# The scan of the linear branch in the causal stage, cut into two halves of 512 columns in consecutive steps

## The reference

```python
qkv = (x @ Wqkv_w + Wqkv_b).reshape(Bb, Ll, 3, Hh, dd)      # 16 heads of 8
...
attn = jax.nn.softmax(scores + causal_mask, axis=-1)
y_softmax = jnp.einsum('bhij,bhjd->bhid', attn, v)
retention = 1.0 - jax.nn.sigmoid(Lambda_raw)
k_stp = k * scale
def step(state, inp):
    q_t, k_t, v_t = inp
    hebbian = v_t[..., :, None] * k_t[..., None, :]
    state = retention * state + Gamma * hebbian
    y_t = jnp.einsum('bhij,bhj->bhi', W_static + state, q_t)
    return (state, y_t)
...
y = alpha * y_softmax + (1.0 - alpha) * y_stp
```

## Time and profile before

| | |
|---|---|
| median of 3 runs | 1887.36 us (1886.95 to 1887.83) |
| the profiled execution | 1888.6 us, span 1887.3 us |
| mean granted clock of TensorE | 0.957 |
| busy: PE, DVE, ACT, POOL | 1647.2, 1276.3, 1113.8, 689.8 us |
| scan L1457 | 32 instructions, 73.8 us |

### The profile page before, as it was taken

How to read it: one execution, slowest core, us unless ns; L and a number is a source line. 1 busy time by engine, 2 the same in 40 slices (tenths; PEclk the granted TensorE clock), 3 DMA queues, 4 the chain that set the end, 5 groups by cost and what they waited for, 6 DMA issues and landing times. The chain is left out here.

```text
span 1887.3 us, 45037 instructions
## 1 busy us (share of the span) xinstructions
PE 1647.2 (87%) x19451; PEld 1016.3 (54%) x19472; DVE 1276.3 (68%) x2067; ACT 1113.8 (59%) x1654; POOL 689.8 (37%) x500
## 2 busy tenths in 40 slices
PE   4588888999999999999997778888888888899999
PEld 2355656777677767776774223333343343466665
DVE  4666746666666667666666868877877886765664
ACT  3265677766776676667662467667666767533221
POOL 4112202443444244424442265565655555411100
PEclk7699999999999999999997799999999999999999
DMA  6764100000000000000015146237226222000000
GB/s 177 201 152 117 28 15 1 2 2 2 1 2 2 2 1 2 2 2 1 2 64 131 36 140 150 69 102 169 69 85 163 69 69 69 23 6 12 6 12 12
DMA packets 38747, 102.27 MB, mean 54 GB/s; under 512 B 3944, under 2 KB 12288, under 8 KB 35284
## 3 DMA queue, kind: packets, MB, share of 16 engines
q1 hardware_dynamic: 37524, 93.09, 18.6%
q10 hardware_dynamic: 1024, 6.29, 1.7%
HBM read 67.12 MB, written 31.46 MB: 52 GB/s over the span
## 5 line engine op out<-in xcount | busy, mean ns | idle before, releaser
L1447 DVE TENSOR_REDUCE arena<-ring 128x2 f32<-128x1024 f32 (+2 forms) x320 | 342.1, 1110 | 89.0 <-PE ring L1304 62.3
L1547 ACT ACTIVATE arena<-ring 128x1024 f32<-128x1024 f32 (+1 forms) x320 | 291.3, 937 | 129.4 <-PE ring L1333 90.2
L1354 PE MATMUL accs<-arena 128*9 128x512 f32 (+3 forms) x1536 | 174.3, 528 | 2.7 <-ACT arena L1547 2.6
L1297 PE MATMUL ring<-arena 48*128 48x512 bf16 (+3 forms) x768 | 127.4, 343 | 42.7 <-DVE arena L1447 21.8
L1326 PE MATMUL ring<-arena 51*128 51x512 bf16 (+3 forms) x768 | 124.1, 341 | 45.6 <-DVE arena L1447 25.5
L2486 POOL TENSOR_TENSOR arena<-arena 128x1280 f32<-128x1280 f32 x28 | 65.3, 2332 | 266.5 <-PE accs L2256 235.1
L2470 POOL TENSOR_TENSOR arena<-arena 128x1024 f32<-128x1024 f32 x32 | 76.1, 2377 | 203.6 <-DVE arena L2346 203.6
L2478 POOL TENSOR_TENSOR arena<-arena 128x512 f32<-128x512 f32 x112 | 142.0, 1303 | 11.3 <-DVE arena L2327 11.3
L292 POOL TENSOR_SCALAR xn<-x,moments,rstd 128x128 f32<-128x128 f32 x80 | 64.3, 817 | 193.9 <-DVE rstd L263 178.3
L2753 ACT ACTIVATE arena<-ring 128x512 f32<-128x512 f32 x80 | 47.8, 597 | 147.3 <-PE ring L2608 140.5
L2713 DVE TENSOR_TENSOR arena<-arena,ring 128x512 f32<-128x512 f32 x80 | 55.0, 687 | 87.9 <-PE ring L2610 74.5
(11 more groups left out here) (345 smaller groups left out, 4269.6 us busy)
## 6 DMA issues: line engine op xcount, KB each, us to landing
arena<-whole_k SPq DMA_DIRECT2D x32, 512.0 KB, 4.7
arena<-whole_q SPq DMA_DIRECT2D x32, 512.0 KB, 6.3
arena<-c_scratch_q SPq DMA_DIRECT2D x14, 384.0 KB, 8.8
arena<-c_scratch_k SPq DMA_DIRECT2D x14, 384.0 KB, 11.9
a_scratch_k<-arena SPq DMA_DIRECT2D x8, 512.0 KB
c_scratch_k<-arena SPq DMA_DIRECT2D x8, 512.0 KB, 3.6
a_scratch_q<-arena SPq DMA_DIRECT2D x4, 768.0 KB, 3.6
arena<-a_scratch_q ACTq DMA_DIRECT2D x8, 384.0 KB, 6.5
```

Of the source, the lines that this page charges most:

```text
L1297: mm = nc.tensor.matmul(o[r], qs[half(r, SCORE), pair, n * P:(n + 1) * P], ks[half(r, SCORE), pair, a:c], start=True, stop=not diag)
L1354: mm = nc.tensor.matmul(acc[ci % 2][32 * h:32 * h + HD + 1, a - c * BANK:BANK], c_values[b % 2][:, j, r * HEADS // 2 + 2 * g + i, :], weig ...
L1447: nc.vector.tensor_reduce(dst, src, AX.X, ALU.max, negate=True).then_inc(c_max_taken.up(item), 1)
L1547: nc.scalar.activation(view(c_probs[wi % 4]), view(ps), ACT.Exp).then_inc(c_weights_made.up(item), 1)
```

## The change

The scan of 1024 columns becomes two of 512 columns. The second starts from the last column of the first, and waits on VectorE for the first to be over. The first stays where the scan was, the second is hung on the following step, in front of what that step already held for the scale. The scale waits for the second half. The planner keeps the old cost for the first half and charges nothing for the second, so the order of all other items is the same. `HALVES` is 2 and `BANK` is 512.

```diff
--- before.py
+++ after.py
@@ -1067,7 +1067,8 @@
                 for j in range(HD):
                     s = at + 6 * j
                     side[s + (j == 0)].append(("kv", b, j))
-                    side[s + 3 + (j == 0)].append(("scan", b, j))
+                    for h in range(HALVES):
+                        side[s + 3 + h + (j == 0)].append(("scan", b, j, h))
                     more = j < HD - 1
                     side[s + 4 + more].append(("scale", b, j))
                     side[s + 5 + more].append(("read", b, j))
@@ -1106,6 +1107,9 @@
                         return 0.00205 * cols, (), 0
                     n = len(score_pairs(c, j)[item[5]])
                     return n * (0.00077 * cols + (0.15 if a == j * P else 0)), (("A", 0.17 + 0.00166 * n * cols),), 1
+                if item[0] == "scan" and item[3]:
+
+                    return 0, (), 0
                 return TIMES.get(item[0], (0, (), 0))
 
             clock = {"P": 0.0, "A": 0.0, "D": 0.0}
@@ -1451,11 +1455,16 @@
                             nc.vector.tensor_tensor(late[:, :, 0, :], late[:, :, 0, :], late[:, :, 1, :], ALU.min).then_inc(
                                 c_max_joined.up((b, g)), 1)
                     elif kind == "scan":
-                        _, b, j = item
+
+                        _, b, j, h = item
                         sk = c_spread["k"][j % 2]
                         dv.wait_ge(c_kv_made, (b, j))
-                        nc.vector.tensor_tensor_scan(sk[:, :], c_retain[:, j:j + 1].to_broadcast([P, T]), sk[:, :], 0.0,
-                                                     ALU.mult, ALU.add).then_inc(c_state_made.up((b, j)), 1)
+                        if h:
+                            dv.wait_ge(c_state_made, (b, j, h - 1))
+                        cols = sk[:, h * BANK:(h + 1) * BANK]
+                        nc.vector.tensor_tensor_scan(cols, c_retain[:, j:j + 1].to_broadcast([P, BANK]), cols,
+                                                     sk[:, h * BANK - 1:h * BANK] if h else 0.0,
+                                                     ALU.mult, ALU.add).then_inc(c_state_made.up((b, j, h)), 1)
                     elif kind == "att":
                         _, b, p = item
                         view = ps[:, :].rearrange("p (n h c) -> p n h c", n=2, c=32)
@@ -1556,7 +1565,7 @@
 
                         _, b, j = item
                         sk = c_spread["k"][j % 2]
-                        ac.wait_ge(c_state_made, (b, j))
+                        ac.wait_ge(c_state_made, (b, j, HALVES - 1))
                         nc.scalar.activation(sk[:, :], sk[:, :], ACT.Identity, bias=w("c_static", j, j + 1),
                                              scale=w("c_gamma", j, j + 1)).then_inc(c_state_scaled.up((b, j)), 1)
                     elif kind == "tp" and item[2] < pairs:
```

## The result

The changed kernel takes 1903.47 us (median of 5 runs, 1899.24 to 1906.45), the kernel before beside it 1887.83 (5 runs, 1886.95 to 1890.93): 1.0059 times as long, with a 95% interval of 1.0038 to 1.0081. Forecast were 1890.4 and a range up to 1896. The loss is some 11 us by the ratio (with 7 to 15 in its interval) and 15.6 by the two medians; 3 were forecast. The profiled execution took 1899.67 us, its span is 1898.4, and the mean granted clock 0.947 against 0.957.

A forecast was written before the change was run, and what follows sets the result against it. It took the handing over of the ring's three PSUM buffers as the causal stage's bound. Batch 0 gave +0.15, batches 1 and 2 +0.40 each, batch 3 +2.04, together +3.0 us: 1890.4 us from 1887.36, range 1884 to 1896.

The forecast's parts named there:

- a half: Each 512-column scan on VectorE: 0.16 us fixed plus 1.06, so 1.22 us; carry read 0 to 0.16, taken as 0.
- adjacent pair: Two halves with nothing between end 2.48 us after the start instead of 2.28: +0.20 us for what waits behind.
- j = 0: First scan of a batch: later second half delays ScalarE's scale; +1.22 us in batches 1, 2, +1.24 in 3, +0.75 in 0.
- j = 1: Adjacent halves in batches 1 and 2: the reduction behind also waits for scores, so only +0.08 us each.
- j = 3, 5: Adjacent halves in batches 0 to 2: scores and ScalarE's scale wait behind the scan, so all of +0.20 us is paid.
- j = 4: GpSimd's cast is freed earlier by the shorter first half; TensorE's transposes of the maxima start 0.5 us earlier.
- j = 6: Same chain through GpSimd's cast: TensorE's transposes of the maxima start 0.8 us earlier, in batches 0 to 2.
- rival (b): Granted clock: three or four more stretches at 1.2 GHz cost 2.5 to 3.5 us, giving 1893.5 us; chance 0.20.
- own sign of being wrong: The prediction would be wrong if, among other signs, stretches at 1.2 GHz changed in number by more than three.
- Rival (a): Delay at j = 0 is absorbed, gains at j = 4 and 6 stay: 1886 us, down to 1883.5; chance 0.16.
- deciding point: Whether TensorE's scores L1297 behind the scale still start within 0.3 us of their old place relative to the scan.
- Rival (c): Gains and losses both end in slack, as VectorE, ScalarE and TensorE are under 85% busy: 1887.4 us; chance 0.22.

The follow-up runs named there:

- odd_only: Kernel before with only the scans of j = 1, 3, 5, 7 in halves, in consecutive steps: 1898.45 us, 1.0040 of before.
- same_j0w: Kernel before with the scans of j = 1 to 7 in halves, both in the same step, j = 0 whole: 1900.28 us, 1.0061 of before.
- j0_only: Kernel before with only the scan of j = 0 in halves, the other seven whole: 1895.25 us, 1.0034 of before.
- delay_small: Kernel before, no scan split, with a 16-column ScalarE copy between scan and scale of j = 0: 1891.92 us, 0.9999 of before.
- same_fill: same_j0w with W score matmuls repeated once or twice more ahead of two idle stretches of TensorE, units 2 and 3: 1895.99 us, 1.0032 of before.
- j46: Kernel before with only the scans of j = 4 and 6 of batches 0 to 2 in halves: 1889.06 us, 0.9996 of before.
- j46_fill: j46 with one W score of unit 3 formed twice more ahead of idle TensorE: 1886.60 us, 0.9976 of before.
- j0_whole: Changed kernel with the scan of j = 0 whole again, the other seven in halves: 1891.95 us, 1.0000 of before.

## Why the prediction was wrong

Point by point, against its own steps. "Measured" is the ledger of a steady batch, of changes that stand in both traces of the changed kernel.

| step | forecast | measured |
|---|---|---|
| a half | 1.22 us, carry read 0 to 0.16 | 1.215 first, 1.28 second half (medians) |
| adjacent pair | +0.20 | +0.25 |
| j = 0 | +1.22 (batch 0 +0.75) | +1.23 (+0.75 and +0.88) |
| j = 1 | +0.08 | +0.25 (+0.08, +0.18) |
| j = 2 | 0 | 0 |
| j = 3, 5 | +0.2 each | +0.25 each |
| j = 4 | -0.5 | -0.48 |
| j = 6 | -0.8 | -0.31 - 0.49, and +0.50 back at vT |
| j = 7 | 0 | 0 |
| sum | +0.40 | +1.2 |

**The direct terms** were read rightly but for j = 1 and the end of j = 6. Behind j = 3 and 5 the carry read shows, about 0.07 us. In rows, two adjacent halves of j = 5:

```profile
1325.64 2.54 DVE L1465 TENSOR_TENSOR_SCAN arena<-arena 128x512 f32<-128x512 f32 x2
```

2.54 against 2.28 for the whole scan. By the Trainium skill (VectorE: DVE Perf Modes, section on the DRAIN), which measured it on tensor_copy, the semaphore between them costs nothing extra; the pair would then cost one fixed part of 0.16 and the carry's 0.07, less 0.08 of overlap, 0.15 us. Measured are 0.26, so here the wait costs 0.11, near the 0.12 that the prediction had from rows 5 and 7.

The step on j = 6 had the right first waits but not the whole chain: half a microsecond of its gain ends at vT, because GpSimd's products set when L1733 runs, and they were not among the rows that I followed. Besides, 0.3 of the 0.8 is not the cast's: before, the join L1451 took 0.60 us there, to the end of a GpSimd product that had begun at 1329.59, and 0.17 after. In odd_only, where j = 6 is whole and the cast takes its 2.24 us, the ledger has the same -0.31. So that the two add up to the forecast 0.8 is luck for 0.3 of it. The Trainium skill, GPSIMD Engine Reference, section Specifications, says that GpSimd's SBUF interfaces are shared with VectorE and contend with instructions of two inputs from SBUF; these rows agree: the join has two such inputs and lasts until the product ends.

The sum of the local terms is about +0.5 in batch 0 (j = 1 can't be read there, the stretches at 1.2 GHz differ), +1.2 in each of 1 and 2, and +1.9 in batch 3 (1.23 for j = 0, 0.25 for j = 1, 0.46 for j = 3; forecast 2.04): +4.8 us for the forecast +3.0. That alone would have been 1892, in the range.

**The step that failed** is the one that kept the clock out of the sum and put it into rival (b) as "three or four more such stretches" at 0.85 us, with a chance of 0.20. By the granted clocks of all runs the changed kernel is at 1.2 GHz for 192 us and the kernel before for 168 to 169: 23 us more, seven stretches of 3.4. With 11 to 13 us of loss by the two ratios and 4.8 of local terms, 6 to 8 us are left for them, 0.9 to 1.2 us each; at the 0.29 us that the executions of one kernel show for 1 us at 1.2 GHz they cost 7 us. So the price was nearly right and the number half of what came; the prediction's own sign of being wrong, a change in number by more than three, came true. Rows 2 and 14 showed stretches at 1.2 GHz in a batch of before, and each place of the batch where the walk found a few tenths of a microsecond was a chance for one more. I had tied them to j = 0 alone. The runs show otherwise: odd_only and same_j0w leave j = 0 whole and have 188 and 192 us at 1.2 GHz, j0_only 174.

At one place the price stands by itself: behind j = 0 of batch 3. The changed kernel has a stretch there that the kernel before has in neither trace. The changed kernel, its copy and before:

```profile
1537.00:1540.40 3.40, 3.40 (x24) 1.18 (x23) 2.15 (x2) 1.23 (x2) 3.12 (x2) 0.50 0.01 2
```

```profile
1538.90:1542.30 3.40, 3.40 (x23) 1.18 (x21) 2.01 (x2) 1.09 (x2) 2.98 (x2) 0.50 0.01 2
```

```profile
1529.50:1532.90 3.40, 3.04 (x34) 1.76 (x26) 2.36 (x5) 2.02 (x5) 1.95 (x1) 1.00 0.02 5
```

In the ledger it costs 1.52 and 1.51 us. delay_small, with a hold of 0.25 us, has it too (+1.56). But so have three of the traces with a whole scan and no hold at j = 0 (same_j0w, same_fill, j46), so the hold isn't what it takes.

Over the fifteen kernels of the table the change against before goes with the mean time at 1.2 GHz, 0.47 us for each us of it (correlation 0.93). That slope holds the local delays too, which grow along with it, so it is no price of the clock by itself (the 0.29 within one kernel is nearer to that). That idle time brings the stretches, and not the other way round, rests on the fills, on the trace of j46_fill above all: three batches of three.

**Rival (a)**, the relief wins: half true and hidden. The gains exist, but in j46 they end as idle TensorE and 1.2 GHz; only with that idle time filled is the median clear of before. Its deciding point, whether L1297 (now L1301) behind the scale starts within 0.3 us of its old place relative to the scan, decided against it: it starts 5.73 us behind the scan's start where it was 4.50, 2.20 behind the scale's both times, so the hold was not absorbed. **Rival (c)**, all ends in slack: false for the change, true for delay_small and j0_whole.

What stays open: why a stretch begins. In j0_whole TensorE idles 1.12 us behind j = 5 of batch 1 as in same_j0w, and keeps 2.4 GHz. I can say at which places stretches came, not foretell them; batches 1 and 2 of one trace can differ in it. Nor is the price fixed: steps of 1.0 to 1.8 us stand in the ledger for one stretch.

## What to carry to other kernels

When the profile of before shows TensorE at 1.2 GHz in every batch, the sum of local terms is only a part of the price of a change: count the stretches at the lower clock in the profile of before, take the number of places that the edit shifts, and carry the clock as a term of the sum with a range of its own, not as a rival. Cutting one instruction in two puts two fixed parts and a wait in the path of whatever stands behind; cut only where a row shows an instruction being held by the long one (here the cast), and follow the gain to the next engine that it ends at. If idle TensorE opens there, try a few repeated matmuls ahead of it: in the traces they kept a loss of 1.3 us a batch away where the gain was 0.8 (in the runs 0.9996 and 0.9976 of before, whose intervals overlap). Then look whether the stretch is gone or only stands further on.

## What the runs showed of the hardware that was not expected

A stretch at 1.2 GHz came behind idle times of TensorE as short as 1.0 to 1.5 us in otherwise busy work, and adding 0.25 us to an idle time of 0.87, or 0.5 to one of 1.02, could bring one. One of the four of a steady batch of before, from 1297.2 us, came behind idle times of no more than 0.57 us:

```profile
1294.47 0.34 PE L1297 MATMUL ring<-arena 48*128 48x384 bf16 x2 [0.35 <-DVE arena L1447]
...
1295.81 0.39 PE L1297 MATMUL ring<-arena 48*128 48x512 bf16 x2 [0.57 <-ACT arena L1547]
1296.72 0.34 PE L1326 MATMUL ring<-arena 51*128 51x384 bf16 x2 [0.52 <-ACT arena L1547]
...
1297.53 0.50 PE L1326 MATMUL ring<-arena 51*128 51x384 bf16 x2 [0.17 <-DVE arena L1447]
```

Work added ahead of an idle time kept a stretch away at its place in all three batches of j46_fill and in both of same_fill at unit 2; behind j = 5 it did so in one batch and moved it by 2 us in the other. The batches with six matmuls more took 149.8 and 155.3 us, those of same_j0w without them 153.3 and 154.9. A scan that takes its start value from a column of memory took 1.28 us where one with an immediate takes 1.215. And the 17 traces, whose kernels are the same up to the causal stage, reach its first exponential up to 16 us apart (3.7 us for the two traces of the kernel before, 4.8 for those of the changed one), with the time at 1.2 GHz in the first 270 us between 51 and 82 us: one trace of each kernel can't tell a change of 0.5% from that.
